# A fused two-layer kernel on one core: the second attention's start, its first three rotations over three engines and the second batch's input work moved inside the first head's first block

## What is computed

```python
q = (hidden_states @ Wq).reshape(b, t, NH, D).transpose(0, 2, 1, 3)
k = (hidden_states @ Wk).reshape(b, t, NKV, D).transpose(0, 2, 1, 3)
v = (hidden_states @ Wv).reshape(b, t, NKV, D).transpose(0, 2, 1, 3)
...
q = q * cos + _rotate_half(q) * sin
k = k * cos + _rotate_half(k) * sin
...
attn = jnp.einsum('bhtd,bhsd->bhts', q, k) * scale
causal = jnp.triu(jnp.ones((t, t), dtype=bool), k=1)
attn = jnp.where(causal, -jnp.inf, attn)
attn = jax.nn.softmax(attn, axis=-1)
out = jnp.einsum('bhts,bhsd->bhtd', attn, v)
out = out.transpose(0, 2, 1, 3).reshape(b, t, NH * D)
return out @ Wo
```

## Time and profile before

| | |
|---|---|
| median of 3 runs | 1020.88 us (1019.99 to 1022.72) |
| the profiled execution | 1022.33 us |
| its span, first to last instruction | 1020.4 us |
| TensorE busy | 929.5 us, 91% of the span |
| VectorE busy | 734.2 us, 72% |
| ScalarE busy | 624.0 us, 61% |
| GpSimd busy | 357.9 us, 35% |
| mean granted TensorE clock | 0.968 |

### The profile page before, as it was taken

One profiled execution on the slowest core, in us unless ns is written; L12 is line 12 of the kernel. 1 busy time (PEld: TensorE's weight loads), 2 busy tenths in 40 slices (PEclk: granted clock), 3 DMA queues, 4 the chain that ended last, 5 costly groups with the idle time before them and its releaser, 6 DMA issues. The chain is left out here.

```text
span 1020.4 us, 16221 instructions
## 1 busy us (share of the span) xinstructions
PE 929.5 (91%) x5608; PEld 536.5 (53%) x5608; DVE 734.2 (72%) x1496; ACT 624.0 (61%) x1247; POOL 357.9 (35%) x401
## 2 busy tenths in 40 slices
PE   3689999999999998986699999999999999988998
PEld 2222222322323224334567677777777776677997
DVE  6899999999999996446745454545454546777887
ACT  3268888888888885422555556555555554355665
POOL 5700000000000000014494939484858472245522
PEclk9789999999999998998799999999999999999999
DMA  3400111010000000000000000000000011000000
GB/s 68 159 25 24 37 43 50 28 48 17 26 21 18 9 1 12 1 0 7 1 4 8 1 6 12 1 1 7 11 1 1 6 54 30 1 1 12 11 12 12
DMA packets 23370, 20.03 MB, mean 20 GB/s; under 512 B 5176, under 2 KB 17440, under 8 KB 23288
## 3 DMA queue, kind: packets, MB, share of 16 engines
q1 hardware_dynamic: 23288, 18.99, 6.3%
HBM read 14.26 MB, written 4.59 MB: 18 GB/s over the span
## 5 line engine op out<-in xcount | busy, mean ns | idle before, releaser
L895 ACT ACTIVATE probs<-score_bank 128x512 f32<-128x512 f32 x512 | 267.8, 601 | 74.6 <-PE score_bank L971 74.4
L759 DVE TENSOR_REDUCE halves<-max_bank 128x2 f32<-128x1024 f32 x256 | 298.6, 1219 | 11.3 <-PE max_bank L931 9.2
L1566 ACT ACTIVATE a_probs<-a_scores,a_lowest 128x896 f32<-128x896 f32 (+7 forms) x128 | 94.9, 742 | 111.0 <-DVE a_lowest L1561 110.3
L1972 PE MATMUL a_sum<-a_turned,a_v 128*128 128x512 f32 (+3 forms) x384 | 158.6, 500 | 1.4 <-ACT a_headsT L1880 1.3
L931 PE MATMUL max_bank<-k_stack,q_stack 48*128 48x512 bf16 x512 | 117.1, 397 | 25.0 <-DVE halves L759 24.8
L984 PE MATMUL summed<-probs,v_tile 128*32 128x512 f32 x1024 | 138.1, 612 | 0.5 <-ACT probs L895 0.5
L971 PE MATMUL score_bank<-q_stack,k_stack 50*128 50x512 bf16 x512 | 132.0, 385 | 4.1 <-ACT probs L895 2.2
L1561 DVE TENSOR_REDUCE a_lowest<-a_scores 128x1 f32<-128x896 f32 (+7 forms) x128 | 96.2, 755 | 37.2 <-PE a_scores L1555 36.6
L686 POOL COPY v_tile<-values 128x128 f32<-128x128 f32 x16 | 4.7, 296 | 303.5 <-PE summed L984 303.5
L1963 PE MATMUL a_turn<-identity,a_probs 128*128 128x128 f32 x576 | 95.6, 275 | 3.1 <-ACT a_probs L1566 2.5
L1797 DVE COPY a_turned<-a_turn 128x512 f32<-128x512 f32 x96 | 57.4, 598 | 51.2 <-PE a_turn L1963 51.0
(11 more groups left out here) (299 smaller groups left out, 1640.1 us busy)
## 6 DMA issues: line engine op xcount, KB each, us to landing
rope<-in_rope SPq DMA_DIRECT2D x8, 256.0 KB, 3.2
rope<-in_L_ffn_mlp_w SPq DMA_DIRECT2D x8, 256.0 KB, 4.3
q_parts<-l_q_parts SPq DMA_DIRECT2D x2, 768.0 KB, 4.9
k_parts<-l_k_parts SPq DMA_DIRECT2D x2, 768.0 KB, 6.3
q_stack<-q_parts SPq DMA_DIRECT2D x30, 48.0 KB
k_stack<-k_parts SPq DMA_DIRECT2D x30, 48.0 KB
x<-in_L_attn_x SPq DMA_DIRECT2D x2, 512.0 KB, 4.3
q_stack<-shift SPq DMA_DIRECT2D x64, 2.0 KB
```

The source lines that it names most:

```text
L759: dve.reduce_max(halves[:, u % 2, half, :].rearrange("p (x t) -> p x t", x=2)[:, :, qt], max_bank[place % RING][:, :, :], AX_X).then_inc(f ...
L895: act.activation(probs[:, step % PROBS, x, :], score_bank[e % SCORES][:, :], ACT.Exp, scale=SCALE0).then_inc(prob_ready, 1)
L1566: act.activation(probs[:, k % 2, c, 0:row_width(n)], scores[n % 2][:, 0:row_width(n)], ACT.Exp, bias=lowest[:, n % 8:n % 8 + 1], accum_out ...
L1972: pe.matmul(sum_bank[:, skipped(k, j):CH], v[:, BLOCKS[k][0], j, :], turned[:, m % SLOTS, skipped(k, j):CH], start=(j == 0), stop=(TURNED_ ...
```

## The change

1. **First three rotations** (units 0, 1 and 3; `URGENT = 3`). VectorE straightens; ScalarE swaps the halves from PSUM; VectorE multiplies by the sines in place, in SBUF; the sum is GpSimd's for the first two, VectorE's for the third; ScalarE takes the high halves; the low halves are VectorE's for the first and third and GpSimd's for the second. The third works in three buffers of `turned`. Rotations 4 to 6 go the usual way. The projections' order becomes 0, 1, 3, 5, 2, 6, 7, 4.
2. **Exponential's table**: an exponential of one column (`touched`) stands at the head of ScalarE's program.
3. **Statistics** of batch 1's first four tiles move to the end of `layer0_mixture`'s VectorE program, before its two low parts; the other four go between the first maxima.
4. **Rows**: ScalarE scales them with the inverse root and an offset (`find_offset`, `scale_row`), where VectorE had normalised them.
5. **Turns of batch 1's rows** go into block 0 of the first head (`READY`), both through `proj_bank`; that head's units of batch 1 start at block 0, j = 5 and so reach into block 2.
6. **Order of the units** in every head is 0, 1, 3, 5, 2, 4, 6, 7, and the first score of each block waits for the rotation that it uses.

```diff
-FIRST_ORDER = [0, 1, 3, 5, 6, 7, 2, 4]
+FIRST_ORDER = [0, 1, 3, 5, 2, 6, 7, 4]
 FIRST_ROTATED = [u for u in FIRST_ORDER if u < NROT]
+UNIT_ORDER = FIRST_ROTATED + [u for u in FIRST_ORDER if u >= NROT]
+READY = {(0, 1): ("turn", NCH // B), (0, 2): ("lower", NCH // B), (0, 3): ("turn", NCH // B + 1), (0, 4): ("lower", NCH // B + 1)}
...
-            units = [(1, u) for u in range(NPROJ)]
+            units = [(1, u) for u in UNIT_ORDER]
...
+            if first and (k, j) in READY:
+                yield "ready", READY[k, j]
-            if units and j % 2:
+            if units and j % 2 and not (first and k == 0 and j <= 4):
...
+    def find_offset(self, dve, b):
+        of = slice(b * TB, (b + 1) * TB)
+        return dve.scalar_tensor_tensor(out=self.moments.root[:, of], in0=self.moments.mean[:, of], scalar=-1.0,
+                                        in1=self.moments.inverse[:, of], op0=ALU.mult, op1=ALU.mult)
+    def scale_row(self, act, x, tile):
+        return act.activation(self.normed[:, tile, :], x[:, tile, :], ACT.Identity, scale=self.moments.inverse[:, tile:tile + 1],
+                              bias=self.moments.root[:, tile:tile + 1])
...
+                dve.wait_ge(added, NCH - 1)
+                a1.take_stats(dve, chain, t.x, TB, TB + 4)
+                a1.aggregate(dve, chain, TB, TB + 4)
...
-                for i in range(DIRECT):
-                    rotate(i)
-                a1.take_stats(dve, chain, t.x, 1)
-                a1.aggregate(dve, chain, 1)
+                straighten_first(0)
+                straighten_first(1)
+                cross_first(0)
+                straighten_first(2)
+                cross_first(1)
+                cross_first(2)
+                straight_part, crossed_part, total = rooms(2)
+                dve.wait_ge(first_crossed, 3)
+                dve.tensor_tensor(total, straight_part, crossed_part, ALU.add).then_inc(third_sum, 1)
+                lower_first(0)
+                lower_first(2)
+                straighten_next(3)
                 take_lowest(0)
+                a1.take_stats(dve, chain, t.x, TB + 4, 2 * TB)
                 take_lowest(1)
...
+                act.activation(touched[:, :], t.identity[:, 0:1], ACT.Exp)
+                for i in range(URGENT):
+                    swap_first(i)
+                for i in range(URGENT):
+                    raise_first(i)
...
+                act.wait_ge(offset_found, 1)
+                scale_rows(FIRST)
...
+                        if what == "ready" and n[0] == "turn":
+                            if n[1] == FIRST:
+                                scale_rows(FIRST + 1)
+                            act.wait_ge(tr_ready, n[1] - FIRST + 1)
+                            a1.raise_in(act, proj_bank[:, :], n[1]).then_inc(tr_out, 1)
...
-                pe.wait_ge(v_taken, from_one(2))
-                pe.wait_ge(swapped_ready, from_one(NROT))
-                for c in range(FIRST, NCH):
-                    pe.wait_ge(normed_ready, c - FIRST + 1)
-                    transpose_tiles(pe, turned_bank[c - FIRST], normed, t.identity[:, :], c).then_inc(tr_ready, 1)
```

More of the change, by code:

```diff
@@ L1366, in use, with attention_order @@
         yield "take", k
-def attention_order(last):
+def attention_order(first, last):
     units, turned = [], []
@@ L1379, in attention_order @@
         if k == 0:
-            units = [(1, u) for u in range(NPROJ)]
+            units = [(1, u) for u in UNIT_ORDER]
         if k == NB // 2:
-            units = [] if last else [(0, u) for u in range(NPROJ)]
+            units = [] if last else [(0, u) for u in UNIT_ORDER]
         placed = None
@@ L1408, in attention_order, with bank_before @@
     yield "close", NB - 1
-def bank_before(last, step):
-    users = [e for e in attention_order(last) if e[0] in ("project", "output") or e[0] == "mix" and e[1][0] in ("turn", "gate")]
+def bank_before(first, last, step):
+    users = [e for e in attention_order(first, last) if e[0] in ("project", "output") or e[0] == "mix" and e[1][0] in ("turn", "gate")
+             or e[0] == "ready" and e[1][0] == "turn"]
     i = users.index(step)
@@ L1531, in swap @@
                 last = act.activation(swapped[to, slot, :], bank[of, :], ACT.Copy)
-            last.then_inc(swapped_ready, 1)
-        def cross(dve, bank, u, slot, count):
-            if count > 2:
-                dve.wait_ge(summed_ready, from_one(count - 2))
-            for half in range(2):
-                to, of = slice(half * 64, half * 64 + 64), slice(64 - half * 64, 128 - half * 64)
-                last = dve.tensor_tensor(swapped[to, slot, :], bank[of, :], table_of(u, 1)[to, :], ALU.mult)
             last.then_inc(swapped_ready, 1)
@@ L1599, in _ @@
                     load_out(g + 1)
-                sp.wait_ge(rotated, from_one(rotations(LAST, 1, NROT - 1)))
+                sp.wait_ge(rotated, from_one(rotations(LAST, 1, FIRST_ROTATED[-1])))
                 for g in range(m1.GROUPS):
@@ L1679, in body @@
                 def body(g, last):
-                    for what, n in attention_order(last):
+                    for what, n in attention_order(g == 0, last):
                         if n == ("stats", 0):
@@ L1789, in body @@
                 def body(g, last):
-                    for what, n in attention_order(last):
+                    for what, n in attention_order(g == 0, last):
+                        if what == "ready" and n[0] == "lower":
+                            dve.wait_ge(tr_out, n[1] - FIRST + 1)
+                            a1.lower_in(dve, proj_bank[:, :], n[1]).then_inc(tr_low, 1)
                         if what == "mix":
@@ L1929, in body @@
                         if what in ("project", "output"):
-                            before = bank_before(last, (what, n))
+                            before = bank_before(g == 0, last, (what, n))
                             if before is not None and before[0] == "mix":
                                 pe.wait_ge(mix_gate_taken, 1)
+                            elif before is not None and before[0] == "ready":
+                                pe.wait_ge(tr_whole, NCH - FIRST)
                             elif before is None or before[0] == "output":
```

212 lines of the change are left out of this document (117 added, 95 removed).

## The result

| | before | after |
|---|---|---|
| median, beside each other on one chip | 1022.01 us (1019.99 to 1023.16, 7 runs) | 1026.38 us (1021.05 to 1026.91, 7 runs) |
| ratio, 95% interval | | 1.0032 (1.0016 to 1.0047) |
| the profiled execution, its span | 1022.33, 1020.4 us | 1021.05, 1019.3 us |
| the same kernel measured twice more (e1, e9) | | 1.0004 (0.9989 to 1.0019), 1.0012 (0.9991 to 1.0033) |

A forecast was written before the change was run, and what follows sets the result against it. It took TensorE's waits and lower clock from 470 to 502 us as all that could be won. The second batch's first projection 2.1 us later, the rest 0: 1020.9 + 2.1 = 1023.0 us, range 1015.4 to 1026.0.

The forecast's parts named there:

- Part 1: First three rotations on three engines, some VectorE operations queueing with GpSimd: first score at 481.3 instead of 482.47, 1.2 us won.
- Part 2: Exponential's table load, and four tiles' statistics in the mixture's tail: 0, or at most 1.7 us if idle cover were gone.
- Part 3: First four scores: TensorE idle 3.9 us before them, so 1.2 GHz for the first 4 us; score 0 ready at 483.7.
- my case: The forecast's own account of the whole change: +0.5 to +4 us, 1021.4 to 1024.9; chance 0.50.
- Part 4: Second batch's root: thirteen small VectorE operations pass one per GpSimd operation, offset at 501.6; 494.05 if none is held.
- two per gap: Rival at the root: two small VectorE operations pass per GpSimd operation, 2.7 us sooner, 1020.3 us; chance 0.12.
- Part 5: Rows, turns and projections inside the first block: second batch's first projection at 514.3, 2.1 us later at equal work.
- Part 6: The rest, including two value projections moved to block 2: 0, with at most 0.3 us waiting for the output's copy.
- The root escapes: Rival at the root: small operations not held by GpSimd, offset at 494.05, rows 7.6 us sooner, 1015.4 us; chance 0.22.
- The clock stays low: Slower rival in the first block: clock still 0.50 beyond 509, 3.1 us more, +5.2, 1026.1 us; chance 0.16.

The follow-up runs named there:

- e1: The changed kernel measured again without any edit; 1025.0 us, 1.0004 against the kernel before.
- e9: The changed kernel measured once more without any edit, on another chip; 1025.79 us, 1.0012 against the kernel before.
- e2: Changed kernel plus one line: GpSimd waits for the root's offset before the fifth rotation; 1020.4 us, 0.9960 against the kernel before.
- e10: Changed kernel with one refinement step in place of three for the second batch's root; 1021.87 us, 0.9978 against the kernel before.
- e3: Changed kernel with the second batch's turns of rows back in their own stretch before block 0; 1024.84 us, 1.0004 against the kernel before.
- e4: Changed kernel with turns in their own stretch before block 0 and GpSimd waiting for the root's offset; 1019.8 us, 0.9959 against the kernel before.
- e7: Changed kernel plus twelve matmuls with overwritten results before the first score; 1023.92 us, 1.0015 against the kernel before.
- e5: Changed kernel with its first four rotations made as in the kernel before; 1024.89 us, 1.0031 against the kernel before.
- e8: Changed kernel with GpSimd waiting for the offset, fourth exponential before the fifth swap, and eighteen added matmuls; 1015.34 us, 0.9936 against the kernel before.
- e11: Changed kernel plus twelve matmuls before the first score and six before the first turn; 1024.95 us, 1.0010 against the kernel before.
- e12: Changed kernel plus eighteen matmuls in two places and GpSimd waiting for the root's offset; 1018.59 us, 0.9940 against the kernel before.

## Why the prediction was right

**Part 1** said 1.2 us won at the first score, with cross, sum and low halves queueing with GpSimd. Measured 1.55 (12.41 against 10.86), with the stretches it named:

```profile
474.18 1.32 DVE L1731 TENSOR_TENSOR a_swapped<-a_swapped,rope 128x512 f32<-128x512 f32 x1
...
476.18 1.64 DVE L1754 TENSOR_TENSOR a_turned<-a_turned 128x512 f32<-128x512 f32 x1
...
478.52 1.57 DVE L1736 TENSOR_TENSOR m_room<-a_turned,m_room 128x512 fp32r<-128x512 f32 x1
```

The mechanism was right, and so was the order: counted from the first projection, the second cross ends at 6.21 us (forecast 6.29), the third at 6.86 (6.89), VectorE's sum at 8.53 (8.74), the last low half at 10.80 (11.19). The price runs both ways: the third cross started first (475.46, 0.69 long), and GpSimd's sum, which started at 475.58, took 1.69 us where the one before it took 1.28. Cross alone takes 0.69, as taken.

**Part 2** said 0, and it is 0: VectorE's idle time before the mixture's low parts shrank from 2.50 us to 1.18, and the first projection came as soon as before (4.97 us behind the last turn of rows, against 4.96). The table's load ended at 469.97, while ScalarE's first swap waited for VectorE until 471.67.

**Part 3** took the first scores at 1.2 GHz; the runs show either level, worth 1.3 to 2.4 us at the fourth output. In e1, where it fell, the root starts at 21.42 after a forecast 21.39. The Trainium skill, "TensorE: Matmul & The Clock Gate", section "What's actually happening", says the cold phase is "run-variable": the same kernel shows different numbers of slow matmuls. The rows above agree: one program shows 0.50 and 0.79 us for the same matmul. The full clock had its place in the forecast as the lower end of my case (+0.5, 1.6 us less), and the fourth output shows 1.3 to 2.4.

**Part 4** is the step that failed: "one per GpSimd operation", read off one row of four 128x128 operations. Two get through, which is the rival *two per gap* that I gave 0.12, and the thirteen take 7.8 to 8.1 us where I had 10.15: 2.3 us too dear in e1. The four of that row were queued at once, and the last two took 1.3 and 1.4 us each; the root's are 8 columns wide and each waits for the one before. Which of the two differences lets the second one through is open. The bounds (2.6 and 10.15) held it. The rest of the part held: the offset gates the rows, the copy and the next maximum, and e2 and e10 show that the root's length passes on almost in full. The Trainium skill, "SBUF — State Buffer", section "SBUF: two separate sides", has the loser block fully until the other's instruction ends; the held operations do end 0.01 to 0.03 us after GpSimd's. But a short one follows each time, starting within the 0.07 us before GpSimd's next or with it, and takes its 0.17. I had cited this as the possible reading and then priced the stricter one.

**Part 5**: four scaled rows were taken at 1.1 us, bounds 0.8 and 1.5:

```profile
496.70 1.65 ACT L296 ACTIVATE normed<-x,a_token_root,a_token_inverse 128x128 f32<-128x128 f32 x4 [5.83 <-DVE a_token_root L292]
```

1.65, outside the bounds. One of them takes 0.48 us (median of eight), where the row that I took as nearest has 0.368, and four in a row start 0.39 us apart: each overlaps the next by only 0.1. From the turn of rows to the first projection I had 11.45 and found 12.21 in e1. At that projection, at equal work (43.44 less the 1.3 us of two projections), the forecast was 2.1 late; e1 is 1.2 late, e9 0.1, the first profile 1.2 early.

**Part 6** said 0, at most 0.3. It is 1.2 in all three profiles: between the second batch's first projection and the fourth output each gives back that much. The two value projections that now stand in block 2 make most of it, as their places show. Two places with the change, then the first of them in the kernel before:

```profile
532.56 0.39 PE L2028 MATMUL a_sum<-a_turned,a_v 128*128 128x128 f32 x2
533.40 1.16 PE L1540 MATMUL a_proj<-a_w_whole,a_inT_whole 128*128 128x128 f32 x8 [0.45 <-ACT a_swapped L1561]
534.39 0.38 PE L2019 MATMUL a_turn<-identity,a_probs 128*128 128x128 f32 x2
...
538.84 1.16 PE L1540 MATMUL a_proj<-a_w_whole,a_inT_whole 128*128 128x128 f32 x8
```

```profile
536.15 0.39 PE L1972 MATMUL a_sum<-a_turned,a_v 128*128 128x128 f32 x2
536.38 0.38 PE L1963 MATMUL a_turn<-identity,a_probs 128*128 128x128 f32 x2
```

The first place took 1.83 us (532.56 to 534.39) where it took 0.23 before, so its projection costs 1.60; the second took 1.89 where it took 0.65, so 1.24. In block 1 before, a value projection cost 0.89 (1.54 against 0.65). That is 1.06 us over for the two, of which 0.45 is the wait for ScalarE's copy of a rotation's halves, which I had not seen; I had put 0.3 on a wait for the output's copy. The rest of the 1.06 has no named wait and stays open. This is read from the timelines and not tested by itself; in e3 and e4, where the units keep their places, the distance to before is constant from the first output on.

**The sum** in e1's steps: 2.1 forecast, less 2.3 for the root, plus 0.6 for the rows, plus 0.8 behind the turn, plus 1.2 in blocks 1 and 2 gives 2.4, which is its measured distance (88.72 less 86.32). So the total was near by luck: one term too dear by 2.3 met three too cheap by 2.6. With the root's length right and all else as forecast, I would have said -0.2. *The root escapes*: false, since every second operation is held; e2 shows that an unheld root is worth 4.6 us by the medians, where the rival had 7.6 against its fully held one. *The clock stays low*: e1's mean of 0.77 from 503 to 515 us is 1.2 GHz until about 508.5, 37.1 us after the first projection. The rival's 509 is 38.9 after it, and its 3.1 us did not come. Two things outside 470 to 550 us moved by over 1 us, which I had put outside my account: the second attention's start and its end near 885 us.

## What to carry to other kernels

Here a chain of tiny VectorE operations beside a GpSimd queue cost 0.6 to 0.7 us a link instead of 0.2. Where such a chain's end gates TensorE and GpSimd's own work has slack, let GpSimd wait for the chain: here that was one line worth 4.6 us, more than the whole change. Read such an edit by a milestone inside its stage, counted from the stage's own start: executions of one kernel spread by 7 us, while the stage's steps can be told 1 us apart. Check then that the stages ahead are not moved by the edit, since such a count hides that. And look at the gaps together: the clock stayed up only where both long ones were closed (7.2 us for both, 4.6 and 0.8 alone, within the uncertainty said above).

## What the runs showed of the hardware

- Two short VectorE operations that wait for each other pass per GpSimd operation: one is held to its end, and the next starts in the 0.07 us before GpSimd's next, or with it, and takes its usual 0.17 us. Held operations with one SBUF input (L118 1.07 us, L120 1.13) behave as those with two (L122 1.12).
- GpSimd is held too: its second sum took 1.69 us, with VectorE's cross started 0.12 us before it; the first took 1.28.
- The clock can fall far from the change. In e1, e3, e7, e9 and e10 the second attention's end loses another 1.56 us near 885 us, in unchanged work; the kernel before, the changed kernel's first profile and e2, e4, e5, e8, e11 and e12 don't. The stretch in e9, then in the first profile, the granted clock eighth:

```profile
868.00:892.00 24.00, 22.95 (x136) 17.18 (x135) 16.43 (x48) 9.21 (x25) 4.99 (x5) 0.93 0.00 1
```

```profile
868.00:892.00 24.00, 21.74 (x133) 15.86 (x132) 17.73 (x61) 9.23 (x25) 6.25 (x6) 1.00 0.01 2
```

What sets it off is open. It adds to the spread of executions. Whether it also occurs in the kernel before, whose executions ran from 1020.37 to 1027.23 us on one chip, its one trace doesn't show.
